# Masked attention and a gated FFN: masks, a layer norm and the fp16 split of one key chunk move to GpSimd

## The reference, cut to what matters

```python
x = x + gnn(layernorm(x))          # x: 4096 x 128, adj: 4096 x 4096 of 0 and 1
x = x + ffn(layernorm(x))

def gnn(x):                        # 2 heads of 64
    q, k, v = x @ Wq, x @ Wk, x @ Wv
    scores = einsum('nhd,mhd->hnm', q / 8, k)
    scores = where(adj > 0, scores, -9e15)
    sat = einsum('hnm,mhd->nhd', softmax(scores), v)
    return leaky_relu(concat(sat[:2048] @ weightr, sat[2048:] @ weightd) + bias, 0.01)

def ffn(x):                        # 8 experts, hidden 256, the best 2 of them per token
    mask = one_hot(top_k(x @ Wg + bg, 2)).sum()
    h = gelu(einsum('td,edh->teh', x, W1) + b1)
    return einsum('ted,te->td', einsum('teh,ehd->ted', h, W2) + b2, mask)
```

## Time and profile before

| | us |
|---|---|
| median of 3 runs | 852.59 (851.79 to 852.61) |
| the profiled execution, its own time | 851.31 |
| its span in the trace | 849.5 |
| PE busy in the span | 811.7 |
| ACT, DVE, POOL busy in the span | 679.0, 639.2, 195.5 |

### The profile page before, as it was taken

One profiled execution on the slowest core, in us unless ns is written; L12 is line 12 of the kernel. 1 busy time (PEld: TensorE's weight loads), 2 busy tenths in 40 slices (PEclk: granted clock), 3 DMA queues, 4 the chain that ended last, 5 costly groups with the idle time before them and its releaser, 6 DMA issues.

```text
span 849.5 us, 31821 instructions
## 1 busy us (share of the span) xinstructions
PE 811.7 (96%) x12080; PEld 597.7 (70%) x12080; DVE 639.2 (75%) x1530; ACT 679.0 (80%) x1099; POOL 195.5 (23%) x209
## 2 busy tenths in 40 slices
PE   4969999999999999999999999999997889999997
PEld 2537777777777777777777777777776567777775
DVE  6597888888888888888888888887883465555555
ACT  4838887878788888878888888788885789999996
POOL 4180000100100010000001000000000566766774
PEclk9979999999999999999999999999999999999999
DMA  8515433443343334434333443443100000000000
GB/s 220 110 25 91 81 58 58 66 74 58 56 77 59 56 61 72 65 56 69 67 56 58 68 71 56 63 72 56 31 0 2 1 14 14 14 14 12 12 12 12
DMA packets 40900, 44.96 MB, mean 53 GB/s; under 512 B 22168, under 2 KB 32160, under 8 KB 40864
## 3 DMA queue, kind: packets, MB, share of 16 engines
q0 software_dynamic: 9216, 33.56, 24.6%
q1 hardware_dynamic: 31216, 10.71, 5.4%
q10 hardware_dynamic: 432, 0.20, 0.1%
HBM read 71.72 MB, written 2.10 MB: 87 GB/s over the span
## 4 chain that ended last, share of the span: by engine, by line
PE 73%; POOL 14%; issue 8%; DVE 3%; DMA 1%; ACT 0%; POOLq 0%; DVEq 0%
PE ps L912 28%; PE ps L881 19%; PE ps L896 19%; POOL prob L349 14%; PE ps L923 2%; PE ps L837 1%; PE ps L842 1%; PE ps L850 1%; DVE prob L589 1%; PE ps L931 1%; PE ps L828 1%; DMA x_sb<-in_x 1%; DVE stats L513 0%; POOLq L348 0%; ACT prob L418 0%
## 5 line engine op out<-in xcount | busy, mean ns | idle before, releaser
L589 DVE CUSTOM_DVE_ANT_0 prob<-ps,mask 128x1024 f32<-128x1024 f32 x256 | 311.8, 1219 | 90.1 <-PE ps L881 84.4
L418 ACT ACTIVATE prob<-prob,nmax 128x1024 f32<-128x1024 f32 x256 | 292.8, 1144 | 9.9 <-DVE nmax L597 9.9
L912 PE MATMUL ps<-pt,v_sb 128*64 128x128 f32 x4096 | 253.2, 277 | 0.0
L912 PEld LDWEIGHTS ps<-pt,v_sb 128*64 128x64 f32 x4096 | 222.4, 137 | 13.4 <-issue 7.5
L433 ACT ACTIVATE pt<-ps 128x1024 f32<-128x1024 f32 x128 | 131.1, 1024 | 113.0 <-PE ps L896 113.0
L896 PEld LDWEIGHTS ps<-ident,prob 64*128 64x128 f32 x4096 | 152.6, 139 | 78.5 <-issue 78.4
L881 PE MATMUL ps<-k_half,q_row 64*128 64x512 f16 x1536 | 189.7, 380 | 5.0 <-DVE low L589 5.0
L896 PE MATMUL ps<-ident,prob 64*128 64x64 f32 x4096 | 183.7, 229 | 9.4 <-issue 4.7
L349 POOL TENSOR_TENSOR prob<-prob 128x512 f16<-128x512 f32 x104 | 122.6, 1183 | 57.1 <-ACT prob L483 54.4
L294 POOL DMA_DIRECT2D mask<-in_adj x64 | 35.4, 553 | 429.2 <-DVE low L589 429.2
L791 DVE SCALAR_TENSOR_TENSOR x_sb<-ps,k_half,x_sb 128x128 f32 (+1 forms) x256 | 72.5, 344 | 78.1 <-PE ps L1029 76.8
(11 more groups left out here) (97 smaller groups left out, 670.8 us busy)
## 6 DMA issues: line engine op xcount, KB each, us to landing
mask<-in_adj POOLq DMA_DIRECT2D x64, 512.0 KB, 5.5
q_row<-q_nat SPq DMA_DIRECT2D x128, 32.0 KB, 4.7
x_sb<-in_x SPq DMA_DIRECT2D x4, 512.0 KB, 7.0
out<-x_sb SPq DMA_DIRECT2D x8, 256.0 KB, 2.3
pt<-in_L_ffn_W SPq DMA_DIRECT2D x1, 1024.0 KB, 6.5
wq_sb<-in_L_gnn_Wq ACTq DMA_DIRECT2D x1, 64.0 KB, 2.9
wk_sb<-in_L_gnn_Wk ACTq DMA_DIRECT2D x1, 64.0 KB, 4.5
wv_sb<-in_L_gnn_Wv ACTq DMA_DIRECT2D x1, 64.0 KB, 5.7
```

Of the source, the lines that this page charges most:

```text
L418: act.activation(prob[:, h, cols], prob[:, h, cols], ACT.Exp, bias=nmax[:, h:h + 1], scale=-1.0, accum_out=sums[:, j, h, p:p + 1]).then_in ...
L589: dve.tensor_tensor_reduce(out=prob[:, h, col_of(p)], in0=ps[:, 2 * (u % 2):2 * (u % 2) + 2, :].rearrange("p b c -> p (b c)"), in1=mask[:, ...
L912: ins = pe.matmul(ps[dims, AV, 0:P], v_sb[:, tile, dims], pt[:, UNITS.index((h, p)), t, :], start=(tile == 0), stop=(tile == NT - 1))
```

## The change

- **Masks on POOL.** `make_mask` leaves DVE. POOL makes the mask in place in 16-bit integers: max with 0, then add -0x2080, which gives the bf16 pattern of a large negative number for 0 and of a tiny positive one for 1.
- **One key chunk in fp16 halves.** For key chunk 1 (`SPLIT_P`, units 1 and 3) ACT copies the transposes to `pt_raw`; POOL writes the high half `pt_hi` and the low half `pt_lo`, 1024 columns each; the values of that chunk are split once. `attend` then multiplies high by high, high by low and low by high: 48 fp16 matmuls in place of 16 in fp32.
- **A layer norm and a residual on POOL.** `inverse_std`, `normalise` and `residual` run there; `leaky` reads PSUM and has two instructions on DVE in place of one.
- **Order.** `AV_BLOCK` is 2. Even units are now the ones copied in halves, odd ones whole by ACT. `divide` and `leaky` stand together behind `mask_scores` of unit 6, `invert_sums` behind unit 4. `x2t_low` and `keep_logits` move to the next odd step. The ranking of the gates moves from between the last two steps into the last one.
- **The start.** The projection to v moves from the start into steps 0 and 1 of PE. The FFN's weights are split in 16 parts, one each even step, with tensor_tensor against a broadcast `factor`.

```diff
+AV_BLOCK = 2
+SPLIT_P = 1
+SPLIT_UNITS = (1, 3)
+WHOLE = (0, 2, 4, 5, 6, 7)
+V_UP = 2.0 ** 5
...
-        pt = sb("pt", [P, NU, KT, P], F32)
+        pt = sb("pt", [P, len(WHOLE), KT, P], F32)
+        pt_raw = sb("pt_raw", [P, 2, KT, P], F32)
+        pt_hi = sb("pt_hi", [P, 2, KT, P], F16)
+        pt_lo = sb("pt_lo", [P, 2, KT, P], F16)
...
+            def make_mask(i, par, c):
+                pool.wait_ge(adj_in[par][c], 8 * i - 8 * par + 16)
+                pool.nop(nofuse=True)
+                part = mask[:, par, c * HALF:(c + 1) * HALF].bitcast(I16)
+                pool.tensor_scalar(part, part, 0, MASKED, ALU.max, ALU.add).then_inc(mask_ready, 1)
...
+            def split_pt(j, u, early=False):
+                q = u // 2
+                pool.wait_ge(pt_by_act, NU * j + u + 1)
+                if not early:
+                    pool.wait_ge(av_done, NP * j + SPLIT_P - 3)
+                pool.nop(nofuse=True)
+                pool.tensor_scalar(pt_hi[:, q, :, :], pt_raw[:, q, :, :], 1.0, 0.0, ALU.mult,
+                                   ALU.add).then_inc(pt_hi_by_pool, 1)
+                pool.wait_ge(pt_hi_by_pool, 2 * j + q + 1)
+                pool.tensor_tensor(pt_lo[:, q, :, :], pt_raw[:, q, :, :], pt_hi[:, q, :, :],
+                                   ALU.subtract).then_inc(pt_by_pool, 1)
...
+            def step(i, par, prior=True, post=True, ahead=True, load=True, split=True, early=False):
+                if ahead:
+                    make_mask(i + 1, 1 - par, 0)
+                if post and par == 0:
+                    inverse_std(i - 4)
+                    normalise(i - 4)
+                if prior:
+                    split_pt(i - 1, 1, early)
+                    split_pt(i - 1, 3, early)
+                if load:
+                    load_adj(i + 2, par, 0)
+                if split and par == 0:
+                    split_ffn_part(i)
+                if ahead:
+                    make_mask(i + 1, 1 - par, 1)
+                if post and par == 1:
+                    residual(i - 3)
+                if load:
+                    load_adj(i + 2, par, 1)
...
+            make_mask(0, 0, 0)
+            make_mask(0, 0, 1)
+            step(0, 0, prior=False, post=False, split=False)
+            split_values()
             pool.wait_ge(w1_in, 16)
-            split_weights(0, w1_raw, w1_pair)
             pool.wait_ge(w2_in, 16)
-            split_weights(1, w2_raw, w2_pair)
+            split_ffn_part(0)
...
                 if p < NP - 1:
                     copy_xnt(2 * p + 2)
                     copy_xnt(2 * p + 3)
-                copy_v(2 * p)
-                copy_v(2 * p + 1)
                 if p < NP - 2:
                     normalise_x(2 * p + 4)
                     normalise_x(2 * p + 5)
+            for j in range(V_FIRST):
+                copy_v(j)
...
+                if u % 2 and prior:
+                    dve.wait_ge(transposed, NU * i - NU + u + 1)
...
+            def leaky(t0, bank=POST):
+                pre = ps[:, bank, :].rearrange("p (t c) -> p t c", t=PAIR)[:, :, 0:D]
+                link = linker(post_chain, POST_STEPS // PAIR * t0 + 4)
+                link(dve.tensor_scalar(o_neg[:, :, :], pre, 0.0, SLOPE, ALU.min, ALU.mult))
+                dve.scalar_tensor_tensor(o_act[:, :, :], pre, 0.0, o_neg[:, :, :], ALU.max, ALU.add).then_inc(post_chain, 1)
...
-            def step(i, par, prior=True, now=True, finish=True, post=True, ahead=True, early=False):
+            def step(i, par, prior=True, now=True, finish=True, post=True, ready=True, early=False, last=False):
                 for u in range(NU):
-                    if prior and u % 2:
+                    if finish and u == 4:
+                        finish_tile(i - 2, par)
+                    if prior and u % 2 == 0:
                         copy_pt(i - 1, u, early)
                     if now:
-                        mask_scores(i, par, u)
+                        mask_scores(i, par, u, prior)
                         if u in (5, 7):
                             row_max(i, u // 7, u)
-                    if u == 1 and finish:
-                        finish_tile(i - 2, par)
-                    if ahead and u in (3, 7):
-                        make_mask(i + 1, 1 - par, u // 4)
                     if post and par == 1:
-                        if u == 1:
+                        if u == 0 and ready:
+                            x2t_low(i - 5)
+                        if u == 2 and ready:
+                            keep_logits(i - 5)
+                        if u == 4:
                             invert_sums(i - 3)
-                        if u == 3:
+                        if u == 6:
                             divide(i - 3)
-                        if u == 5:
                             leaky(i - 3)
-                        if u == 7:
-                            residual(i - 3)
                     if post and par == 0:
-                        if u == 1:
+                        if u == 0:
                             statistics(i - 4)
-                        if u == 3:
-                            normalise(i - 4)
-                        if u == 5:
-                            x2t_low(i - 4)
-                        if u == 7:
-                            keep_logits(i - 4)
+                    if last and u == 2:
+                        rank_gates(0, 0, RANKED_EARLY)
...
+                if p == SPLIT_P:
+                    pe.wait_ge(pt_by_pool, 2 * j + 2)
+                else:
+                    pe.wait_ge(pt_by_act, NU * j + ready)
+                    pe.wait_ge(pt_by_dve, copies_by_dve(j, ready))
                 if p == 0 and not first:
                     pe.wait_ge(sat_ready, j)
+                if isinstance(j, int) and j == 0:
+                    pe.wait_ge(v_ready, 2 * p + 2)
                 pe.nop(nofuse=True)
+                if p == SPLIT_P and first:
+                    pe.wait_ge(v_lo_ready, 1)
                 for t in range(KT):
                     tile = p * KT + t
-                    for h in range(HEADS):
-                        dims = slice(h * DH, (h + 1) * DH)
-                        ins = pe.matmul(ps[dims, AV, 0:P], v_sb[:, tile, dims], pt[:, UNITS.index((h, p)), t, :],
-                                        start=(tile == 0), stop=(tile == NT - 1))
+                    if p == SPLIT_P:
+                        for values, probs in ((0, pt_hi), (0, pt_lo), (1, pt_hi)):
+                            for h in range(HEADS):
+                                dims = slice(h * DH, (h + 1) * DH)
+                                ins = pe.matmul(ps[dims, AV, 0:P], v_pair[:, values, t, dims], probs[:, h, t, :],
+                                                start=False, stop=False)
+                    else:
+                        for h in range(HEADS):
+                            dims = slice(h * DH, (h + 1) * DH)
+                            ins = pe.matmul(ps[dims, AV, 0:P], v_sb[:, tile, dims],
+                                            pt[:, WHOLE.index(UNITS.index((h, p))), t, :],
+                                            start=(tile == 0), stop=(tile == NT - 1))
...
+                    if not prior:
+                        project_v(k)
+                    if not prior and k == 3:
+                        project_v(k + 1)
                     if prior:
                         transposes(i - 1, 2 * k + 1, early)
-                    if post and par == 1 and k == 1:
+                    if early and k < NC - V_FIRST:
+                        project_v(V_FIRST + k)
+                    if post and par == 1 and k == 2:
                         out_project(i - 3)
-                    if post and par == 0 and k == 2:
-                        x2_transpose(i - 4)
-                    if post and par == 0 and k == 3:
-                        logits(i - 4)
                     if k >= AV_BLOCK and prior:
                         attend(i - 1, k - AV_BLOCK, early)
                     elif k < AV_BLOCK and drain:
                         attend(i - 2, k + NP - AV_BLOCK)
+                    if post and par == 0 and k == 3:
+                        x2_transpose(i - 4)
+                    if post and par == 1 and k == 0 and ready:
+                        logits(i - 5)
```

More of the change, by code:

```diff
@@ L337, in _ @@
-            for i in range(2, 6):
-                load_adj(i, i % 2)
-            pairs(pool, 6, NT, load_behind_post)
-            for t0 in range(NT - 6, NT, PAIR):
-                inverse_std(t0)
+            pool.tensor_scalar(wrd[:, :, :, :], wrd[:, :, :, :], 1.0 / V_UP, 0.0, ALU.mult, ALU.add).then_inc(w_split_chain, 1)
+            step(1, 1, post=False, early=True)
+            step(2, 0, post=False)
+            step(3, 1)
+            pairs(pool, 4, NT - 2, step)
+            step(NT - 2, 0, load=False)
@@ L343, in ffn @@
+            step(NT - 1, 1, load=False, ahead=False)
+            step(NT, 0, load=False, ahead=False, split=False)
```

(1 more changed line is left out.)

221 lines of the change are left out of this document (130 added, 91 removed).

## The result

| | before | after |
|---|---|---|
| median of 4 runs each, us | 852.19 (851.21 to 852.61) | 1055.74 (1054.76 to 1057.03) |
| ratio, 95% interval | | 1.2391 (1.2372 to 1.2409) |
| span of the profiled execution, us | 849.5 | 1053.1 |
| mean granted clock, profiled | 0.989 | 0.912 |

What follows compares the result with a forecast made beforehand. The prediction took PE, busy 96% of the span, as the bound. Its terms, -12.8 + 16.5 + 0 - 5.6 + 3.9 = +2.0 us on a median of 852.6, gave 854.6 us, range 836 to 870.

Steps and rivals of the forecast that it cites:

- Masks, norm and splits on POOL (0): Loop: work moved to POOL is worth 0 us; POOL needs 14.4 of 18.4 us a tile, a mask taking 1.90.
- rival 3: Loop: POOL becomes the bound or its splits come late for PE, 10 to 20 us more, 865 to 875; chance 0.11.
- fp16 chunk: `attend` on PE: chunk 1 in fp16 takes 1.50 us, saving 0.40 a tile, -12.8 us in all.
- Rival 2: `attend`: fp16 pairs keep one load after another at 0.109 us a pair, giving 895 us; chance 0.05.
- the estimate of 2.7 us: `attend`: by the skill's load rules the fp16 chunk would take 2.7 us and the program 26 us more.
- Wait behind unit 6: Group 3 of odd steps: DVE work between maskings of units 6 and 7 delays PE 1.1 us, +16.5 us in all.
- Start: Program start: the v projection moves into steps 0 and 1, so step 2 begins at 68.7 instead of 74.33; -5.6 us.
- End: Program end: an extra `attend`, the ranking inside the last step and a longer last chain, less shorter groups; +3.9 us.

Runs made afterwards that it cites:

- e8_mult_add_alone: The kernel before, with only the masks of tiles 2 to 31 moved to GpSimd, made by multiply and add: 852.08 us, ratio 1.0002.
- e12: The changed kernel with multiply-add masks and `leaky` behind unit 7's masking, v blocks four and four in steps 0 and 1 instead of five and three: 852.05 us.
- e5_mult_add_masks: The changed kernel with GpSimd's mask made in bf16 by multiply and add instead of max and add: 851.56 us, ratio 0.999.
- e3_int_masks_alone: The kernel before, with only the masks from tile 2 on moved to GpSimd, in integers by max and add: 910.93 us, ratio 1.0696.

## Why the prediction was wrong

**The step that failed** is "Masks, norm and splits on POOL (0)", in its sentence "I take 1.90, the row of the same size and one input". The row was a multiply and add; the mask is a max and add. The size and the number of inputs matched, the operation did not, and the operation decides: 7.09 us, 3.7 times as much. The upper end, 4.07, was the nearest row of another kind and no bound either: the new operation stood in no row of the trace, and two rows of cheap operations say nothing of how dear it can be. With 7.09 in the forecast's own sum, 14.4 + 2 x 5.19 = 24.8 us of GpSimd in a tile; measured were 25.05 (half of 50.09), and (25.05 - 18.68) x 32 = 203.8 us. So rival 3 was the right mechanism with a chance of 0.11; its price, 10 to 20 us, was a twentieth to a tenth of the real one, through the same figure for the mask.

**Masks at 0, had they been cheap: right.** Alone, with multiply and add, the term is +0.2 us (-0.7 to +1.0, `e8_mult_add_alone`), and the changed kernel runs at 851.56, 3.0 under the forecast of 854.6. That agreement is partly luck:

| term | forecast | with cheap masks |
|---|---|---|
| fp16 chunk, PE's own time | -12.8 | -14.1 (16 x 0.88) |
| groups of PE otherwise | 0 | -14.7 (16 x 4 x (0.08 + 0.15)) |
| waits in odd steps | +16.5 | +27.4 (not measured: what is left of a pair, 1.71) |
| loop in all | +3.7 | -1.4 (16 x (37.26 - 37.35)) |
| start (to step 2) | -5.6 | -1.8 |
| end | +3.9 | +3.7 |
| sum | +2.0 | +0.5, on spans +0.4 |

**fp16 chunk: right in mechanism and size.** 0.055 us a pair was the row to take (48 matmuls in 1.46 us, at full clock three pairs every 0.17). Rival 2 is not what this kernel shows, and neither is the estimate of 2.7 us. That one took the load rule of the Trainium skill (TensorE: Matmul & The Clock Gate, LDWEIGHTS) and put a pair's two loads one behind the other, 107 ns. The 2.77 us of the changed kernel come close to both by chance, at half the clock. What arrives of it at the end of the program is another number, 0.41 to 0.74 of 0.88 a pair.

**Wait behind unit 6: right in place, too small.** VectorE's times were right to 0.24 us. The sum took 4.50 for PE's groups, and they shrank to 4.34; in a stretch that VectorE bounds, each tenth that PE gains comes back as waiting. The listed waits are 0.76 + 0.53 a pair, the rest of the 1.71 is in no listed wait; the chain has pieces there that it calls issue, time in which the engine waits for nothing that the profile shows. Only with division and leaky part in the even step did the gain stay.

**Start: too large a gain**, -1.8 for -5.6. Step 2's transposes stand at 72.6 (forecast 68.7, before 74.33). ACT's fifth copy of v and the exponentials behind it hold PE's first transposes until 53.32, and step 1 hands back what comes earlier (`e12`).

**End: right.** From the start of the last masking (632.5 before, 629.2 with cheap masks) to the end of the span it is 217.0 and 220.7. Its dearest piece, the ranking inside the last step (forecast: a wait of 4.7), reads in the timeline of `e5_mult_add_masks`:

```profile
644.06 1.12 PE L996 MATMUL ps<-ident,prob 64*128 64x64 f32 x16 [5.04 <-DVE pt L708]
```

Not settled: why PE's transposes of the odd units take 0.49 us to the next `attend` and not 0.58 to 0.66 as before. The units copied whole and in halves have changed places, and `attend` runs two chunks behind; no run here parts the two. That other pairs of operations are slow on GpSimd is measured, the inner reason is not.

## What to carry to other kernels

Price an operation that moves to another engine by a row with the same engine and the same operation; where there is none, the upper end is open, and one instruction tried by itself is worth more than the whole sum. When an engine looks relieved, add up each queue stretch by stretch, from one fixed point to the next: a wait that is moved along within a stretch that is too long is only handed on, and work has to leave the stretch. Look also at what runs beside a long instruction of the other engine: in `e3_int_masks_alone` GpSimd had time to spare, and its mask still cost 59 us through VectorE's norm. And before giving up an idea that lost 200 us, look for the same result in another form: here multiply and add for max and add, then two short pieces of work moved half a step, made 1055.7 into 840.6.

## What was unexpected of the hardware

On GpSimd, one scalar-operand instruction over 2048 columns cost 1.90 us for multiply and add or multiply and multiply, 5.36 to 5.38 for any single operation tried (multiply, add, max, greater-than), and 7.08 to 7.10 for the other pairs (max and add, less-or-equal and multiply, subtract and multiply, multiply and max), the same in int16, int32, bf16 and fp32 where tried. Adding a harmless second operation to a lone multiply makes it 3.5 us shorter. The Trainium skill (GPSIMD Engine Reference, Engine selection) calls one-input operations on GpSimd roughly line-rate; multiply and add agrees, at 0.93 ns a column, and max and add, at 3.46, does not. Two fp32 inputs on 1024 columns were 2.34 us for add and for multiply alike.

A VectorE instruction of 0.34 us took 2.73 to 5.05 us beside a GpSimd mask of 7.08 us and ended with it (`e3_int_masks_alone`), and 0.34 again beside masks of 1.9 (`e8_mult_add_alone`), while maskings and copies on VectorE kept their 1.22 and 0.69 us beside either.
